# Filling the operand stack of a cross attention from SBUF on ScalarE's DMA queue, with per-stage semaphores and a reordered feed-forward start

## What is computed

```python
x = x + self_attention(layernorm(x))          # 16 heads of 128, gated, with 64 slots
x = x + cross_attention(layernorm(x), ctx)    # per sequence: 256 channels, 16 heads of 16, 512 x 512
x = x + feed_forward(layernorm(x))            # 512 -> 1408 -> 512, SiLU gate, NF4 weights
# cross attention, per head:
q = Wq @ target + bq; k = Wk @ source + bk; v = Wv @ source + bv
dot = mask * (q.T @ k) / 4 - (1 - mask) * 1e6
out = v @ (softmax(dot) * mask)
```

## Time and profile before

| what | value |
|---|---|
| median of 3 runs | 2402.73 us (2401.16 to 2409.71) |
| the profiled execution | 2406.03 us, its span 2404.3 us |
| self attention | 0 to 1479.6 us |
| cross attention | 1479.6 to 2093.6 us |
| feed-forward | 2093.6 to 2404.3 us |
| busy share: PE, DVE, ACT, POOL | 91%, 67%, 33%, 32% |

### The profile page before, as it was taken

The page is one execution under the profiler, slowest core; times in us unless marked ns, Lnnn a source line. Parts: engine busy times, 40 slices in busy tenths (PEclk is TensorE's granted clock), DMA queues, the critical chain, the costliest instruction groups (busy, mean ns, idle before and its releaser), DMA issues. The chain is left out here.

```text
span 2404.3 us, 35495 instructions
## 1 busy us (share of the span) xinstructions
PE 2189.0 (91%) x11638; PEld 1535.4 (64%) x11638; DVE 1602.9 (67%) x2880; ACT 791.9 (33%) x1836; POOL 761.2 (32%) x532
## 2 busy tenths in 40 slices
PE   6899999999998999999999994988888887589998
PEld 4677778777776787778878772333332332167777
DVE  6668788788875568878878853687676876342221
ACT  1313323322332322332232320355444555432221
POOL 3334434533533433433443332112211220112122
PEclk9999999999999999999999996798898998669999
DMA  5211101101102201101110025765556643201100
GB/s 192 85 39 51 37 26 50 56 7 56 50 33 71 97 2 57 50 19 44 50 56 7 28 47 143 121 125 117 117 94 121 133 106 79 87 35 53 53 35 18
DMA packets 58838, 159.05 MB, mean 66 GB/s; under 512 B 9615, under 2 KB 24407, under 8 KB 52215
## 3 DMA queue, kind: packets, MB, share of 16 engines
q1 hardware_dynamic: 57142, 155.82, 24.9%
q10 hardware_dynamic: 1600, 2.02, 0.2%
HBM read 115.09 MB, written 34.33 MB: 62 GB/s over the span
## 5 line engine op out<-in xcount | busy, mean ns | idle before, releaser
L1627 DVE TENSOR_REDUCE x_mx<-x_pm 128x1 f32<-128x512 f32 x512 | 315.9, 679 | 108.4 <-PE x_pm L1720 107.2
L1490 ACT ACTIVATE x_E<-x_pd 128x512 f32<-128x512 f32 x512 | 265.4, 603 | 216.5 <-PE x_pd L1734 215.8
L1084 PE MATMUL a_pj<-q_big,a_wqk_h 128*128 128x512 f32 x1024 | 290.0, 405 | 1.0 <-POOL a_wqk_l L634 1.0
L1100 PE MATMUL a_pj<-a_wvg_h,q_big 128*128 128x512 f32 x1024 | 286.1, 406 | 1.1 <-DVE a_rm L790 1.0
L1100 PEld LDWEIGHTS a_pj<-a_wvg_h,q_big 128*128 128x128 f32 x1024 | 185.3, 188 | 51.8 <-DVE a_rm L790 2.4
L1084 PEld LDWEIGHTS a_pj<-q_big,a_wqk_h 128*128 128x128 f32 x1024 | 182.9, 188 | 40.4 <-POOL a_wqk_l L634 1.5
L790 DVE TENSOR_TENSOR a_rm<-a_pj,a_rope 128x1024 f32<-128x1024 f32 x128 | 155.7, 1217 | 79.4 <-PE a_pj L1084 78.1
L526 ACT ACTIVATE a_v<-a_pj 128x256 f32<-128x256 f32 x128 | 49.1, 384 | 416.0 <-PE a_pj L1100 416.0
L666 POOL TENSOR_TENSOR a_ogl<-a_ogf,a_ogh 128x512 fp32r<-128x512 f32 x64 | 81.7, 1298 | 286.6 <-ACT a_ogf L562 286.6
L1748 PE MATMUL x_pa<-x_E,x_vx 128*32 128x512 f32 x1024 | 149.8, 660 | 0.0
L862 DVE TENSOR_TENSOR a_acc<-a_po,a_acc 128x512 f32<-128x512 f32 x128 | 85.9, 687 | 93.7 <-PE a_po L1213 93.7
(11 more groups left out here) (215 smaller groups left out, 4573.5 us busy)
## 6 DMA issues: line engine op xcount, KB each, us to landing
a_qk_raw<-in_wqk SPq DMA_DIRECT2D x16, 1024.0 KB, 5.5
a_vg_raw<-in_wvg SPq DMA_DIRECT2D x16, 1024.0 KB, 4.9
q_big<-parts_scratch SPq DMA_DIRECT2D x36, 256.0 KB
a_wo_raw<-in_wo SPq DMA_DIRECT2D x16, 512.0 KB, 3.7
x_Q<-parts_scratch SPq DMA_DIRECT2D x30, 256.0 KB
x_K<-parts_scratch SPq DMA_DIRECT2D x30, 256.0 KB
parts_scratch<-x_hi SPq DMA_DIRECT2D x14, 512.0 KB, 2.6
parts_scratch<-x_lo SPq DMA_DIRECT2D x14, 512.0 KB, 3.3
```

What stands on the lines that cost most here:

```text
L1084: last = mm(pj[:, j % 2, :], wa[:, c, j * P:(j + 1) * P], xa[:, c, p * UT:(p + 1) * UT], start=k == 0, stop=k == 11)
L1100: last = mm(pj[:, tt % 2, :], xa[:, c, t0:t0 + P], wa[:, c, :], start=k == 0, stop=k == 11)
L1490: nc.scalar.activation(E[:, n % ESLOTS, :], pd[:, n % 3, :], ACT.Exp, scale=XD ** -0.5).then_inc(exp_done, 1)
L1627: nc.vector.reduce_max(mx[:, u % 2, at:at + 1], pm[:, k % 3, :], AX_X).then_inc(pm_done, 1)
```

## The change

1. `parts_scratch`, `put`, `put_part` and their semaphores are gone. `fill_part` reads the tiles of the halves in SBUF (64 partitions of 4 KB) and writes them to the same 16 partitions.
2. In the cross attention's loop the fills move from SP's to ACT's queue. Batch b + 2 is filled in G = 8 to 15 of batch b (batch 1 in G = 0 to 5 of batch 0). VectorE's first projection of a batch waits until the stack filled from the previous content of the halves has landed. `high` and `take_projection` lose their waits for the stores.
3. Each stage has its own semaphores. POOL clears those of the stage before within the next stage (after `values(1, 1)`, and after `prepare(0)` in the feed-forward); the clearing blocks between stages are gone.
4. Feed-forward: the identity for x comes on ACT's queue; x of the first group is loaded in two halves; w1 and w2 turn through two pairs of banks (`pa`, `pb`); DVE takes 7 tiles of w2, ACT the other 15 of w1 and w2; x is transposed between them; w3's 11 tiles are turned in the first `step`, one after each f, through `po`, and taken by ACT.

```diff
-def fill_part(dma, tile, w, e, seg, split_dram, sem):
+def fill_part(dma, tile, w, e, seg, halves, sem):
     z = slice(64 * e + 16 * seg, 64 * e + 16 * seg + 16)
-    dma(tile[z].bitcast(F32),
-        split_dram[ORDERS[w][seg], w, 64 * e:64 * e + 64].rearrange("(r j) o t -> r (j o) t", j=4)).then_inc(sem, 16)
+    dma(tile[z].bitcast(F32), halves[ORDERS[w][seg]][64 * e:64 * e + 64, 2 * w:2 * w + 2].bitcast(F32)).then_inc(sem, 16)
...
-            put(0, cq_out)
+            def fill(tile, w):
+                for seg in range(3):
+                    part = ORDERS[w][seg]
+                    sp.wait_ge((chi_done, clo_done)[part], 2 * w + 2)
+                    for e in range(2):
+                        fill_part(sp.dma_start, tile, w, e, seg, (xhi, xlo), stack_0)
...
-            sp.wait_ge(cq_out, 32)
...
+            fill(Q0, 0)
             store(1, 0)
-            put(1, ck_out)
-            sp.wait_ge(ck_out, 32)
...
+            fill(K0, 1)
             store(1, 1)
...
-        FILLS = [(0, (2,)), (0, (3,)), (0, (4, 5)), (1, (0, 1)), (1, (2,)), (1, (3,)), (1, (4, 5))] + 9 * [(0, ())]
+        FILLS = 8 * [(0, ())] + [(0, (0, 1)), (0, (2, 3)), (0, (4, 5)), (1, (0, 1)), (1, ()), (1, (4, 5)), (1, (2,)), (1, (3,))]
...
+            def stack(b, w, pieces):
+                for k in pieces:
+                    part = ORDERS[w][k // 2]
+                    act.wait_ge((hi_done, lo_done)[part], 4 * (b - 1) + 2 * w + 2)
+                    fill_part(act.dma_start, (Q, K)[w][b % 3], w, k % 2, k // 2, (hi, lo), stack_in[b % 3])
...
+                    if t < 4:
+                        stack(1, *SECOND[G])
+                    if t // 4 + 2 < B:
+                        stack(t // 4 + 2, *FILLS[G])
...
+            clear(pool, spent)
...
-                    after(dve, (q_split, k_split)[j // 2], 32 * (b - 1))
+                    if j == 0 and b > 1:
+                        dve.wait_ge(stack_in[(b - 1) % 3], stacked(b - 1))
...
+            for r in range(FT):
+                turn(0, r)
+                turn(1, r)
+                if r == MIXED:
+                    pe.wait_ge(ident_done, 16)
+                if r >= MIXED:
+                    transpose_x(0, r - MIXED)
+            transpose_x(0, 3)
...
+                    if isinstance(g, int) and g == 0:
+                        turn_w3(f)
+                if isinstance(g, int) and g == 0:
+                    pe.wait_ge(w3_taken, FT)
...
+            for r in range(BY_DVE - 2):
+                take(r)
             norm_stats(0)
+            for r in range(BY_DVE - 2, BY_DVE):
+                take(r)
             normed(0, 0)
             normed(0, 1)
```

More of the change, by code:

```diff
@@ L102, in sems, with clear @@
         return self.used
-def clear(nc, semaphores):
-    with nc.Block() as block:
-        @block.gpsimd
-        def _(pool):
-            for sem in semaphores:
-                pool.sem_clear(sem)
+def clear(pool, semaphores):
+    for sem in semaphores:
+        pool.sem_clear(sem)
 ORDERS = ((0, 0, 1), (0, 1, 0))
@@ L1438, in _ @@
             rows(0)
-            for w in range(2):
-                for part in range(2):
-                    put_part(1, w, part)
             mask_rows(1, 0)
@@ L1455, in _ @@
                         store(t // 2 - 2)
-                    if b + 1 < B:
-                        stack(b + 1, *(FILLS if b else SECOND)[G])
                     if t == 0 and q == 2:
@@ L1901, in step @@
                         high(g + 1, tt)
-            for tt in range(4):
-                high(0, tt)
+            for r in range(FT):
+                take(0, r)
+                if r >= BY_DVE:
+                    take(1, r)
+                if r >= MIXED:
+                    high(0, r - MIXED)
+            high(0, 3)
             step(0, True)
@@ L1914, in norm_stats @@
             def norm_stats(g):
-                dve.wait_ge(x_in, 16 * g + 16)
-                after(dve, rstd_done, g)
+                first = isinstance(g, int) and g == 0
+                if first:
+                    dve.wait_ge(x_first, 16)
+                else:
+                    dve.wait_ge(x_in, 16 * g + 16)
+                    dve.wait_ge(rstd_done, g)
                 for tt in range(4):
+                    if first and tt == 2:
+                        dve.wait_ge(x_in, 16)
                     V.bn_stats(stats[:, tt, :], xt[:, tt, :]).then_inc(stat, 1)
@@ L1971, in step, with take @@
                     add(g, tt)
+            def take(r):
+                dve.wait_ge(w12_ready, 2 * r + 2)
+                V.tensor_copy(w2[:, :, r * P:(r + 1) * P], spread(turned(1, r))).then_inc(taken_dve, 1)
+            for r in range(BY_DVE - 2):
+                take(r)
             norm_stats(0)
+            for r in range(BY_DVE - 2, BY_DVE):
+                take(r)
             normed(0, 0)
             normed(0, 1)
-            for t, (i, cols, dst) in enumerate(TILES):
-                if t % 2 == 1:
-                    dve.wait_ge(w_ready, t + 1)
-                    src = pa[:, t % 2, 0:256].bitcast(BF16)
-                    V.tensor_copy(dst, src.rearrange("p (q n) -> p q n", q=4)).then_inc(taken_dve, 1)
-            for pair in range(2):
-                if pair:
-                    normed(0, 2)
-                    normed(0, 3)
-                for tt in (2 * pair, 2 * pair + 1):
-                    low(0, tt)
+            low(0, 0)
+            normed(0, 2)
+            low(0, 1)
+            normed(0, 3)
+            low(0, 2)
+            low(0, 3)
             step(0, True)
@@ L2052, in _ @@
             step(G - 1, False)
-    clear(nc, s.used)
+    with nc.Block() as block:
+        @block.gpsimd
+        def _(pool):
+            clear(pool, signals.used)
 def decoder(nc, a, out):
```

137 lines of the change are left out of this document (62 added, 75 removed).

## The result

The changed kernel takes 2420.07 us (median of 10 runs, 2411.88 to 2428.72), the kernel before, run beside it, 2405.13 (2398.53 to 2418.15). The ratio is 1.0059, 95% interval 1.0036 to 1.0083: slower by 0.6%, where 2309 us and faster by 4% were forecast. The profiled execution took 2425.0 us, its span 2423.2.

A forecast was written before the change was run, and what follows sets the result against it. No engine was full on average; TensorE waited in the cross attention for stacks whose fills SyncE issued late, behind maxima. Gains 59.6 + 16.7 + 2.6 + 14.4 = 93.3 us gave 2312.7 profiled, 2309 on the median; range 2290 to 2345.

The forecast's parts named there:

- The wait for the stack goes: Cross attention: TensorE's row scores no longer wait 31.8 us for the next batch's stack, as fills are issued earlier.
- become shorter with the backlog: Cross attention: waits for maxima, left out of the 48 us reading of the loop's gain, were said to shrink.
- Rival 1: Cross attention: maxima stay late on shared engines; TensorE waits 8 us a batch, 2356 us, milder form 2330; chance 0.12.
- An idle microsecond costs 1.5: Cross attention, step 8 of batch 3: price of TensorE idle time including slow products, 8.9/5.85, giving 48 us from waits.
- The ideal batch, 60.7 us: Cross attention: ten steps of 3.15 us and six of 4.86; five batches save 12.5 each, with batch 6 78 at most.
- The term 65: Cross attention loop: gross gain of 65 us, taken between readings of 48 and 78, before costs of 2.4 and 3.
- ScalarE's issues, 2.4 us (0 to 19): Cross attention: ScalarE issues 84 fills at 0.46 us; most hide in idle time, costing 2.4 us in all.
- Rivals 2 and 3: ScalarE's issues on the path, 19 us, 2326 (chance 0.12); ScalarE's queue backs up, 30 us slower than before, 2433 (0.03).
- DVE's new wait in batch 0, 3 us (0 to 6): Cross attention, batch 0, G = 5: DVE waits until stack 1 has landed, costing 3 us.
- Rival 4: Cross attention: stalls only move; DVE's new wait in G = 5 costs 6 us in six batches, 2345 us; chance 0.05.
- The borders, 16.7 and 2.6: Stage borders: next stage after self attention starts 16.7 us sooner, second border 2.6 us shorter, with 0.3 for engines meeting.
- The feed-forward, 14.4 (10 to 18): Feed-forward's start: first product 20.3 us sooner, at 22; w3 tiles cost 5 and x transposes 0.9, net 14.4 us.

The follow-up runs named there:

- no_fills: Changed kernel without the fills of batches 3 to 7, which are computed from the stacks of earlier batches: 2333.8 us in one run.
- planned: Changed kernel with fills thinned out around the maxima, load_x behind them, load_c in mid-batch, batch 1's fills begun before the loop: 2305.4 us.
- loop_undone: Changed kernel with the cross attention loop's fills put back through DRAM on SyncE's queue at their old steps: 2355.7 us.
- fills_on_sp: Changed kernel with the loop's same fills at the same steps issued by SyncE instead of ScalarE: 2383.6 us.
- rows_first_lag: Changed kernel with maxima sent ahead of the spreads of weighted sums, and DVE's reciprocals of the sums moved by up to two steps: 2383.3 us.
- quiet_load_later: Changed kernel with fills moved to steps 10, 11, 14, 15, 2, 3, maxima ahead of the spreads, load_x behind step 13's maxima: 2400.9 us.
- sp_load_later: Changed kernel with the loop's fills issued by SyncE and load_x moved from step 12 to behind the maxima of step 13: 2388.5 us.

## Why the prediction was wrong, point by point

- **The wait for the stack goes.** Right: 31.8 us of it are gone, step 8 fell from 14.2 to 6.2 us, and batch 6 takes 50.4 us, the figure of the prediction's ideal.
- **The maxima's waits "become shorter with the backlog".** This step failed. TensorE's waits for maxima grew from 8.7 us in the kernel before (4.2 for x_Q, 4.5 for q_big) to 56.5. The prediction counted what stands ahead on SyncE's own queue and let the other queue run beside it. The queues share the engines by turns, a turn of the fills being a whole fill long: the maxima of step 9 took 6.8 to 9.2 us in batches 0 to 5, and 2.2 before (batches 2 to 5). The backlog before stood in the middle of a batch, whose steps are 4 to 5 us long, and there the 9.9 us hardly made `dot` wait, though they held up the fills. After, it stands where the maxima are awaited 12.6 us after the start of step 9 (4.8 + 4.9 + 2.9, steps 9 to 11) and 9.2 us after that of step 13 (`no_fills`), and they need 15.5 to 15.8 us there and back at the first and, in batches 0 to 4, 13.0 to 14.7 at the second. The page "DMA: Bandwidth & Descriptors" of the Trainium skill, section "Queues, rings and completion order", has the engines alternate between queues, a packet of descriptors at a time. The prediction took it as speaking for the change; the 9.1, 6.7 and 4.8 us and the windows of packets agree with the page in the alternation, which speaks against the change.
- **Rival 1 named the mechanism and the steps (12 and 0) and was priced too low**, 8 us a batch and chance 0.12. Its durations were right (15 us there and back; 15.5 to 15.8 and 13.0 to 14.7 measured), and so nearly was the wait (56.5 us in six batches, 9.4 each). It counted those us bare and left out the clock: a batch came to 84.0 us (batches 1 to 5), 20.7 above the 63.3 without fills.
- **An idle microsecond costs 1.5.** This failed too, and it is why the loss outran every rival but the third. It was read from one wait, inside step 8, after which the clock was back by step 9. Over batches 2 to 5 the changed kernel has 43.4 - 21.4 = 22.0 us more idle time than `no_fills` and is 83.3 us longer: 3.8 per idle microsecond. The same sum for the kernel before gives 22.3 and 40.6: 1.8. So the price is no constant. It went with where the wait stands; what sets it isn't shown.
- **The ideal batch, 60.7 us.** Measured 63.3: five batches could give 49 us and not 62.5, and with batch 6 the most to be had was 49 + 15.6 = 65, not 78. The term 65, taken as a cautious middle, was thus the ceiling; `planned` gains 50.3 us on `loop_undone`.
- **ScalarE's issues, 2.4 us (0 to 19).** One lasts 0.55 to 0.61 us, beside the exponentials. Against `no_fills`, `planned` has step 8 longer by 0.3 (6.2 for 5.9) and step 11 by 0.5 to 0.7 (3.4 to 3.6 for 2.9) in four of batches 1 to 5, which bounds the issues at about 1 us a batch, 6 in all. Between the changed kernel and `fills_on_sp` steps 8 to 10 differ by 0.3 us at step 8 (6.2 for 5.9) and by 0.1 or less at the others. Rivals 2 and 3 are out.
- **DVE's new wait in batch 0, 3 us (0 to 6).** Too small: step 6 takes 12.1 us for 4.9, with one wait of 7.6 us by DVE for the last fill. Rival 4 is out: no such wait in later batches.
- **The borders, 16.7 and 2.6.** Measured 15.8 (the self attention's last store came 1.6 us later, or it would be 17.4) and 3.2. No row gave the 0.3 us for the meeting of the engines; from the last store's issue to the next stage it took 2.45 us at the second border, for the 3.1 counted.
- **The feed-forward, 14.4 (10 to 18).** Undersized: 22.2. Its first product came 18.4 us after the stage's start, and not 22, as the timeline of TensorE shows, and what it paid for that was 1.7 us net (42.3 - 18.4 - 22.2), for the 5.9 counted:

```profile
2153.04 1.73 PE L2049 MATMUL f_pa<-q_big,f_w 128*128 128x512 f32 x4 [1.50 <-DVE f_xl L1939]
```

```profile
L2023 PE MATMUL f_po<-f_identb,w_raw x44: 219/221/271, 2158.4 to 2198.6; 128*128 128x128 bf16 x44
```

  Each of the 44 w3 products lasts 0.22 us at full length, under 1 us a tile with overlap; the stage's granted clock went from 0.90 to 0.96, and the 1.7 us hold that gain as well, so the price of the w3 tiles alone isn't shown.

- **Two slips that changed nothing.** The name x_Q in the earlier trace rows covers two of the three pairs of stacks, not one (q_big is the third). And the two bounds named for the lower end of the forecast's own range give 2295 us, not 2292.

The forecast time was nearly met by a kernel that was not the one forecast, `planned`, with 2305.4 us for 2309. That is luck and no support for the sum: its feed-forward gives 8 us more than its term and its loop 9 less.

## What to carry to other kernels

A transfer that is moved to a second queue doesn't leave the way of the first: count, for each small transfer that the critical engine awaits, how many of its own queue stand ahead of it, and add a big transfer of the other queue for each and for the transfer itself; do so for the way there and for the way back. Put big transfers where the critical one has slack, and not only where their data are ready. And price an idle stretch by the clock in the steps behind it, not by its own length: two kernels with the same idle time in batches 2 to 5 differed by 14.5% there.

## What the runs showed that was not expected

Two spreads, one and none ahead of 8 KB on the same queue made its landing take 9.1, 6.7 and 4.8 us with fills in flight, and 2.2 with two ahead and no fill in flight. After the waits of step 15 the granted clock stayed at 0.50 for 15 to 30 us of the next batch (batches 0 to 4), but in batches 1 to 5 of the kernel before it came back within step 8, the step of the wait. In batch 6 of the kernel before, waits in steps 7 and 8 were followed by 24 us at 0.50, so the place alone does not decide it. What does wasn't tried and stays open. Taking one wait away made the kernel slower twice (`rows_first_lag`, `quiet_load_later`) and no faster once (`sp_load_later`), since another transfer then came late.
